# Cross attention with a recurrent layer behind it: score steps of a light kind, the second norm in the same iteration, the shift ahead of the spread on the queue

## The reference

```python
q, k, v = x @ Wq + bq, ctx @ Wk + bk, ctx @ Wv + bv       # heads of 8
attn = softmax(q k^T / sqrt(8) + mask)
x = norm(concat(attn v) @ Wo + bo + x) * gamma + beta
xa = ln1(x); sx = previous row of xa - xa
xxx = tanh((xa + sx * maa_x) @ maa_w1)                    # 5 x 32 wide
xk, xw, xv, xr, xg = xa + sx * (maa_stack + xxx @ maa_w2)
w = exp(-exp(time_decay + tanh(xw @ td_w1) @ td_w2))
r, k, v, g = xr @ Wr.T, xk @ Wk.T, xv @ Wv.T, silu(xg @ Wg.T)
def step(s, (r, k, v, w)):                                # over 256 tokens
    a = outer(k, v); return a + w * s, r @ (u * a + s)
x1 = x + (groupnorm(out) * gn_w + gn_b) * g @ Wo.T
xc = ln2(x1); sx2 = previous row of xc - xc               # the second norm
rr = sigmoid((xc + sx2 * ffn_maa_r) @ Wfr.T)
kk = relu((xc + sx2 * ffn_maa_k) @ Wfk.T) ** 2
return x1 + rr * (kk @ Wfv.T)
```

## Time and profile before

| what | value |
|---|---|
| three runs, median (lowest to highest) | 1322.82 us (1318.57 to 1328.49) |
| the profiled execution's own time | 1320.78 us |
| its span, first to last instruction | 1319.0 us |
| PE busy in the span | 1055.0 us (80%) |
| ACT busy | 867.8 us (66%) |
| DVE busy | 633.2 us (48%) |
| POOL busy | 295.0 us (22%) |
| granted clock of PE, mean | 0.919 |

### The profile page before, as it was taken

The page is one execution under the profiler, slowest core; times in us unless marked ns, Lnnn a source line. Parts: engine busy times, 40 slices in busy tenths (PEclk is TensorE's granted clock), DMA queues, the critical chain, the costliest instruction groups (busy, mean ns, idle before and its releaser), DMA issues.

```text
span 1319.0 us, 18192 instructions
## 1 busy us (share of the span) xinstructions
PE 1055.0 (80%) x7100; PEld 388.9 (29%) x7100; DVE 633.2 (48%) x1113; ACT 867.8 (66%) x953; POOL 295.0 (22%) x333
## 2 busy tenths in 40 slices
PE   3067788888898989989898989898988789876654
PEld 1022222332333323322333233332332234213412
DVE  5313122565454735384366536474547334734373
ACT  1047888767776788768776777678866888683001
POOL 6103104121221304130413032230413011301130
PEclk9579999989988999889999998899999999898766
DMA  6543213270326123341327131703241022200210
GB/s 188 127 130 101 62 52 78 44 134 11 85 66 132 25 75 85 50 105 52 72 53 139 41 60 61 143 15 87 72 69 30 2 40 39 44 1 0 42 31 10
DMA packets 65565, 87.47 MB, mean 66 GB/s; under 512 B 8208, under 2 KB 48192, under 8 KB 65472
## 3 DMA queue, kind: packets, MB, share of 16 engines
q1 hardware_dynamic: 63536, 82.91, 29.3%
q0 software_dynamic: 1936, 3.32, 0.9%
HBM read 50.74 MB, written 18.62 MB: 53 GB/s over the span
## 4 chain that ended last, share of the span: by engine, by line
PE 48%; ACT 16%; issue 15%; DVE 15%; POOL 3%; DMA 1%; SPq 1%; ACTq 0%; POOLq 0%; DVEq 0%
PE psum L708 47%; ACT probs L647 13%; DVE vs L1274 2%; DVE row_max L1161 2%; DVE vs L1281 2%; DVE mask_max L1156 1%; DVE k_stack L1491 1%; DVE tmp L1422 1%; ACT L647 1%; DMA vs<-v_c 1%; DVE xa L1248 1%; SPq L328 1%; DMA q_stack<-q_stacked 1%; POOL k_rest L500 0%; DVE sx L1253 0%
## 5 line engine op out<-in xcount | busy, mean ns | idle before, releaser
L647 ACT ACTIVATE probs<-psum 128x1024 f32<-128x1024 f32 (+1 forms) x832 | 797.3, 1024 | 314.7 <-PE psum L708 312.8
L708 PE MATMUL psum<-probs,v_aug 128*9 128x512 f32 (+1 forms) x3328 | 421.3, 618 | 1.1 <-ACT probs L647 0.9
L708 PE MATMUL psum<-q_stack,k_stack 64*128 64x512 bf16 (+1 forms) x1664 | 279.7, 393 | 135.1 <-ACT probs L647 95.6
L708 PEld LDWEIGHTS psum<-q_stack,k_stack 64*128 64x128 bf16 (+1 forms) x1664 | 65.4, 95 | 439.8 <-ACT probs L647 338.4
L708 PEld LDWEIGHTS psum<-probs,v_aug 128*9 128x9 f32 (+1 forms) x3328 | 71.6, 91 | 202.3 <-issue 177.0
L552 POOL TENSOR_TENSOR vs<-r_c,vs 128x512 f32<-128x512 f32 x64 | 84.0, 1318 | 151.6 <-DVE r_c L1418 78.4
L1161 DVE TENSOR_REDUCE row_max<-psum 128x8 f32<-128x1024 f32 x64 | 78.0, 1218 | 59.0 <-PE psum L708 57.7
L1281 DVE TENSOR_TENSOR_SCAN vs<-w_c,vs 128x514 f32<-128x514 f32 x64 | 100.3, 1567 | 12.0 <-POOL vs L543 10.1
L535 POOL TENSOR_TENSOR xm<-tmp,xa 128x512 f32<-128x512 f32 x40 | 46.0, 1166 | 247.9 <-DVE tmp L1268 247.9
L522 POOL TENSOR_TENSOR rstd<-moments,eps 128x2 f32<-128x2 f32 x24 | 4.9, 206 | 311.2 <-DVE moments L1234 311.1
L1208 DVE COPY o_raw<-psum 128x512 f32<-128x512 f32 x32 | 22.1, 689 | 102.8 <-PE psum L708 102.8
(11 more groups left out here) (175 smaller groups left out, 1089.1 us busy)
## 6 DMA issues: line engine op xcount, KB each, us to landing
vs<-v_c SPq DMA_DIRECT2D x64, 257.0 KB, 7.2
ctx_t<-in_mask SPq DMA_DIRECT2D x8, 1601.0 KB, 6.6
k_stacked<-k_parts SPq DMA_DIRECT2D x48, 200.1 KB
k_stack<-k_stacked SPq DMA_DIRECT2D x32, 300.2 KB, 6.6
ctx_t<-in_ctx_t SPq DMA_DIRECT2D x24, 400.0 KB, 5.2
q_stacked<-q_parts SPq DMA_DIRECT2D x96, 64.0 KB, 2.0
q_stack<-q_stacked SPq DMA_DIRECT2D x32, 192.0 KB, 7.3
ctx_t<-in_ctx_t SPq DMA_DIRECT2D x8, 401.0 KB, 3.6
```

Of the source, the lines that this page charges most:

```text
L647: nc.scalar.activation(probs[turn_step % NP][t][0:w, :, :], ps[t][0:w, :, :], ACT.Exp).then_inc(exped.sem, 1)
L708: return nc.tensor.matmul(dst, lhsT, rhs, start=start, stop=stop)
```

## The change

Four things are altered. (1) In the pairs that begin at a step of `LIGHT` (2, 8, 10, 18, 38, 42, 48), and in iteration 0 in all pairs but the first and those of `DIVIDED`, each weighing stands between the two score tiles of its step, where before both stood between the steps. (2) The second norm is done at the end of the iteration of `c`: PE turns `xn` at step 48 and multiplies by `Wfr` at step 50, POOL takes `root(c, 2)` last, DVE forms `xr2` and then `xk2`; `Wfk` follows at step 0 of the next iteration, relu and square on ACT at step 2, `Wfv` at step 6. What is left in `side` moves two steps ahead (four for `Wfv`), on ACT too: `h` from 14 to 12, `Wv` from 18 to 16, `Wr` from 26 to 24, `Wo` from 46 to 44, the queries from 48 to 46. The rounds of `b` move from steps 12 to 15 to 9 to 12, those of `a` by one. DVE's order follows. (3) On SP `shift_to_stack` of half 1 stands right behind `shift_to_dram`, ahead of `spread_v`. (4) `first_state` works on two states at a time, `read_out` waits for `rk`, and DVE makes state pass 3 before `r_c` and `rk`. The number of matmuls, exponentials and DMAs does not change. The core of the diff (the step numbers that only go down by two are left out):

```diff
 KV_SECOND = (5, 6, 5, 6)
...
-B_ROUNDS = [12, 13, 14, 15]
+KV_STEP = [30, 32, 40, 40]
+A_ROUNDS = [31, 32, 33, 34]
+B_ROUNDS = [9, 10, 11, 12]
 
 
...
-                        if step == 18 and b is not None:
+                        if step == 16 and b is not None:
                             shift_to_dram(b, 1)
-                        if step == 20 and c is not None:
+                            shift_to_stack(b, 1)
+                        if step == 18 and c is not None:
                             spread_v(c)
-                        if step == 20 and b is not None:
-                            shift_to_stack(b, 1)
...
-                j0, j1 = HD // 2 * part, HD // 2 * (part + 1)
+                j0, j1 = 2 * part, 2 * part + 2
...
+                pool.wait_ge(rk_ready.sem, rk_ready.at(c))
                 for j in range(HD):
-                    if j == 2:
-                        first_state(c, 1)
+                    if j in (2, 4):
+                        first_state(c, j // 2 + 1)
                     pool.wait_ge(s_ready.sem, s_ready.at(c, j + 1))
...
                     f, a, b, c, d = elements(it, lo)
-                    if d is not None:
...
                         first_state(c, 0)
+                        first_state(c, 1)
                         mixed(c, 4)
...
+                    if c is not None:
+                        root(c, 2)
...
-                    if step == 6:
+                    if step == 2:
                         act.wait_ge(kk_done.sem, kk_done.at(d))
-                        nc.scalar.activation(kk_relu[:, :, :], halves(6), ACT.Relu).then_inc(kk_relued.sem, 1)
+                        nc.scalar.activation(kk_relu[:, :, :], halves(7), ACT.Relu).then_inc(kk_relued.sem, 1)
...
-                    if step == 10:
+                    if step == 0:
                         act.wait_ge(rr_done.sem, rr_done.at(d))
-                        nc.scalar.activation(rr_tanh, halves(7), ACT.Tanh, scale=0.5).then_inc(rr_ready.sem, 1)
+                        nc.scalar.activation(rr_tanh, halves(6), ACT.Tanh, scale=0.5).then_inc(rr_ready.sem, 1)
...
-                if d is not None and step == 0:
-                    pe.wait_ge(xn2_ready.sem, xn2_ready.at(d))
-                    if a is not None:
-                        pe.wait_ge(q_scaled.sem, q_scaled.at(a))
-                    turn_rows(xn, 7, xt2_turned)
                 if c is not None:
-                    if step == 2:
-                        if d is not None:
-                            pe.wait_ge(std_ready.sem, std_ready.at(d))
+                    if step == 0:
+                        pe.wait_ge(o_normed.sem, o_normed.at(c, 3))
                         turn_output(c, 3, 5)
...
-                    elif step == 6:
+                    elif step == 4:
                         pe.wait_ge(attn_kept.sem, attn_kept.at(c))
                         product_rows(attn_t, w_o, 5, wo_done)
-                    elif step == 14:
+                    elif step == 10:
+                        pe.wait_ge(xn_ready.sem, xn_ready.at(c))
+                        turn_rows(xn, 5, xt_turned)
...
+                    elif step == 48:
+                        pe.wait_ge(xn2_ready.sem, xn2_ready.at(c))
+                        if f is not None:
+                            pe.wait_ge(q_scaled.sem, q_scaled.at(f))
+                        turn_rows(xn, 7, xt2_turned)
+                    elif step == 50:
+                        pe.wait_ge(xr2_ready.sem, xr2_ready.at(c))
+                        pe.wait_ge(x1_ready.sem, x1_ready.at(c))
+                        product_rows(xr2, wsq["Wfr"], 6, rr_done)
                 if d is not None:
-                    if step == 4:
+                    if step == 0:
                         pe.wait_ge(xk2_ready.sem, xk2_ready.at(d))
-                        pe.wait_ge(x1_ready.sem, x1_ready.at(d))
-                        product(wsq["Wfk"], xk2, 6, kk_done)
-                    elif step == 8:
-                        pe.wait_ge(xr2_ready.sem, xr2_ready.at(d))
+                        product(wsq["Wfk"], xk2, 7, kk_done)
...
+                        pe.wait_ge(kk_ready.sem, kk_ready.at(d))
+                        pe.wait_ge(rr_ready.sem, rr_ready.at(d))
                         if a is not None:
                             pe.wait_ge(v_kept.sem, v_kept.at(a, 1))
...
-                        product_rows(xr2, wsq["Wfr"], 7, rr_done)
-                    elif step == 10:
-                        pe.wait_ge(kk_ready.sem, kk_ready.at(d))
-                        if a is not None:
-                            pe.wait_ge(v_kept.sem, v_kept.at(a))
                         product_rows(kk_c, wsq["Wfv"], 6, ff_done)
-                if c is not None and step == 10:
-                    pe.wait_ge(xn_ready.sem, xn_ready.at(c))
-                    turn_rows(xn, 5, xt_turned)
...
+                        light = step in LIGHT or (c is None and step > 0 and step not in DIVIDED)
                         if b is not None:
                             score_tile(b, step, 0, general)
+                            if light:
+                                weigh(b, step - 2)
                             score_tile(b, step, 1, general)
                         score_rows(step - 1, it, lo, general)
                         if step == 0:
                             if c is not None:
                                 weigh(c, STEPS - 2)
                                 weigh(c, STEPS - 1)
-                        elif b is not None:
+                        elif b is not None and not light:
                             weigh(b, step - 2)
                             if step not in DIVIDED:
                                 weigh(b, step - 1)
                         if b is not None:
                             score_tile(b, step + 1, 0, general)
+                            if light:
+                                weigh(b, step - 1)
                             score_tile(b, step + 1, 1, general)
                         score_rows(step, it, lo, general)
...
-                dve.wait_ge(s_begun.sem, s_begun.at(c, 2 * j // HD + 1))
+                dve.wait_ge(s_begun.sem, s_begun.at(c, j // 2 + 1))
...
-                    if d is not None:
-                        scaled_rows(xn, x1, d, 2).then_inc(xn2_ready.sem, 1)
...
@@ -1345,53 +1344,50 @@
                             see_mask(a, 1)
                     if c is not None:
                         keep_output(c, 3)
-                    if d is not None:
-                        dve.wait_ge(xt2_turned.sem, xt2_turned.at(d))
-                        token_differences(d, 0, 7, "ln2_w", "ln2_b")
-                        shift_mix(xk2, "ffn_maa_k", xk2_ready)
-                        shift_mix(xr2, "ffn_maa_r", xr2_ready)
-                    if c is not None:
                         norm_output(c, 3, 5)
-                    if it > lo and a is not None:
-                        keep_v(a, 0, 7)
-                    if c is not None:
                         dve.wait_ge(attn_turned.sem, attn_turned.at(c))
                         nc.vector.tensor_copy(attn_t[:, :, :], halves(5)).then_inc(attn_kept.sem, 1)
+                    if it > lo and a is not None:
+                        keep_v(a, 0, 6)
+                        if not general:
+                            see_mask(a, 0)
+                    if c is not None:
                         dve.wait_ge(xb_ready.sem, xb_ready.at(c))
                         dve.wait_ge(wo_done.sem, wo_done.at(c))
                         nc.vector.tensor_tensor(x0[:, :, :], halves(5), x_rows[:, :, :], ALU.add).then_inc(x0_ready.sem, 1)
                         dve.wait_ge(x0_ready.sem, x0_ready.at(c))
                         row_moments(x0, c, 0)
-                    if it > lo and a is not None:
-                        keep_v(a, 1, 6)
-                    if c is not None:
                         link(scaled_rows(x0, x0, c, 0))
...
+                    if it > lo and a is not None:
+                        keep_v(a, 1, 7)
+                    if c is not None:
                         row_moments(x0, c, 1)
+                    if d is not None:
+                        write_out(d)
                     if it == B and not general:
                         count_over()
                         raise_flag()
...
-                    if it > lo and a is not None and not general:
-                        see_mask(a, 0)
-                    if d is not None:
-                        write_out(d)
+                    if b is not None:
+                        reduce_step(b, 1, 0, general)
+                        reduce_step(b, 1, 1, general)
                     if c is not None:
                         dve.wait_ge(xt_turned.sem, xt_turned.at(c))
                         token_differences(c, 1, 5, "ln1_w", "ln1_b")
+                    if b is not None:
+                        reduce_step(b, 1, 2, general)
+                    if c is not None:
```

(17 more changed lines are left out.)

136 lines of the change are left out of this document (64 added, 72 removed).

## The result

The changed kernel takes 1244.23 us (median of four runs, 1242.85 to 1248.33), the kernel before in the same session 1324.08 (1318.57 to 1328.49): a ratio of 0.940, 95% interval 0.936 to 0.945. The forecast was 1245.

A forecast was written before the change was run, and what follows sets the result against it. PE was taken to set the pace, busy 127.8 of 143.1 us; terms sum to -7.75 us per full iteration and 78 us overall, giving 1245 us. The forecast's own range was 1228 to 1262, the wider one 1212 to 1284.

The forecast's parts named there:

- queue wait: PE's wait at the first score tile of step 26, for a small transfer queued behind the spread, goes: -4.55 us.
- clock: Slow matmuls behind PE's gaps cost 3.2 us an iteration; half of one 1.6 us stretch stays: -2.4 us.
- exponentials and split tiles: In light pairs PE's waits for exponentials fall from 8.8 to 5.1 us (-3.7); fewer split tile pairs and gaps give -1.0.
- DVE and POOL: New PE waits for norms, rounds of b, h and mixes make 6.2 us against 1.1 + 1.1 + 0.1 before: +3.9.
- The rule on initiating a DMA: On SP's queue, initiation is usually small relative to the DMA, so queue place would be worth nothing; 14.92 us speaks against it.
- (a): DVE from k_c's copy to the second output norm: waits 0.8 and 1.2 us; rk's 1.96 gain and scan 4's 1.4 to 2 loss count zero.
- (c): Second norm at the iteration's end, Wo to r_c, against PE's 11.9 us before Wfr: 0 counted, 2.8 us upper end.
- the slower rival: PE meets Wfr at step 50 with the 16.6 us chain bare seven times: a loss of 38, 1360 us; chance 0.04.
- Iterations: Gains by iteration: 0, 10 us; 1, 9.5; 2 to 5, 31; 6, 9; 7, 12; the end 6.5.
- Rival 1: DVE's idle time covers the new waits, costing 2 rather than 6.2 us in six iterations: 1220 us; chance 0.2.
- rival 2: DVE and POOL become the bound between steps 9 and 14 and 24 and 30: +28, 1273 us; chance 0.17.
- Rival 3: The step 26 wait was not the queue's place, or another load takes its turn: 43 back, 1288 us; chance 0.06.

The follow-up runs named there:

- the queue alone: The kernel before with only the shift's transfer to the stack rows issued right behind its way to DRAM, ahead of the eight spread DMAs: 1281.98 us, 0.969.
- relu behind step 4: The changed kernel with ACT's relu and square of the second half behind the tiles of step 4 instead of light pair 2: 1243.95 us, 0.939.
- the root ahead of the keys: The changed kernel with POOL's two roots for c put ahead of the key split: 1261.75 us, 0.953.

## Why the prediction held, step by step

The number was right within a microsecond, and that is partly luck: of its terms, several were off and cancelled. The range and the chain of causes held; the closeness says little. For a full period (third one, in us):

| term | forecast | measured | from |
|---|---|---|---|
| queue wait | -4.55 | -4.2 to -4.4 | "issue" 5.5 to 5.7 before, 1.3 with the queue alone |
| clock | -2.4 | about -4.6; mean of iterations 1 to 7: -2.3 | PE busy 127.8 to 123.25, queue alone |
| exponentials and split tiles | -4.7 | -2.8 | 136.60 without light pairs, 133.80 with |
| DVE and POOL | +3.9 | +2.3 | 1.1 of new waits with the queue alone; 1.2 from all else of the change, 136.60 less 135.36 |
| sum | -7.75 | -9.3 | 143.1 to 133.8 |

- **The queue.** The mechanism was right: the transfer stood behind the spread, and in the kernel before its place alone is worth 42 us, against 43 by the forecast's terms. The step that failed is "the spread itself is not delayed ... that distance does not change". The distance that mattered was from the spread to step 26, and in the changed kernel, where `Wv` comes two steps earlier, it is 5.7 us longer. I credited the whole wait to the queue's order, and in the changed kernel that order is worth nothing (1243.37 with it undone). The total came out right because the wait can be removed only once.
- **The rule on initiating a DMA.** The queue's place alone took 42 us off the kernel before, and nothing off the changed one. The Trainium skill, "DMA: Bandwidth & Descriptors", section "Issuing engines are not separate DMA queues", calls the time to initiate a DMA usually small relative to the DMA itself. Read as the prediction read it, both would be nothing; the 42 us do not agree with that, since eight issues in a row add up to 14.9 us.
- **The clock.** Mis-sized for this period: I kept half of one slow stretch for the new small gaps, and there was none. The granted clock was 1.00, with waits of 0.57 to 1.20 still in it. But the same small waits can have a slow stretch behind them. Behind the waits of 1.03 and 0.52 in the second period, and of 1.03 and 0.53 in the third, stand these weighings:

```profile
341.91 2.96 PE L710 MATMUL psum<-probs,v_aug 128*9 128x512 f32 x16
...
475.25 1.91 PE L710 MATMUL psum<-probs,v_aug 128*9 128x512 f32 x16
```

  Over iterations 1 to 7 the queue's edit alone took 16.3 us off PE's busy time, 2.3 each, so on the mean the term was right. The term for split tiles (-1.0) does not show: in a period without a slow weighing or `mix`, PE is busy for 123.25 us with the queue alone and for 125.18 in the changed kernel, presumably because light pairs split rows too.
- **Exponentials.** The waits themselves were forecast at 5.1 and are 3.6 in eight (8.8 before). The two largest, 1.03 and 0.53 behind pair 2, stand where the prediction put 1.75. The period gained less than the waits fell: without light pairs the exponentials' waits are 7.5, and of the 3.9 less, 1.1 came back as waits for row maxima.
- **DVE and POOL.** `Wr` 0.8 and the projection 1.2 were forecast; 0.76 and 1.20 came, which agrees with the count of DVE's work in a row. The rounds of `b`, `h` and the mixes were put at 3.7 and sum to 2.5 (0.57, 0.68, 0.27, 0.19, 0.29, and 0.52 for ACT). The root began right behind the key split, as forecast (484.80), and DVE waited 4.39 for it, where the forecast had it 3.2 late (its own figures, 23.5 less 20, give 3.5). What I left out is why the key split is late: POOL idles 4.23 us for the rows of `x` in front of it, and 4.16 in the kernel before, where it could have been read.
- **(a) `rk` and scan 4.** Counted as zero. `rk` takes 0.87 instead of 2.84, as read; scan 4 waits 2.42 for POOL's first state, more than the 1.4 to 2 counted.
- **(c) `Wfr`.** No wait in the full periods, so the slower rival had no ground. Only the last one, in the end, waits 2.81 for its input.
- **Iterations.** Iteration 0 was forecast at -10 and gave -9.5 (light pairs are all of it: 202.71 without them). Iterations 1 to 7 gave 58.5 for 61.5, with the four full ones better (34.1 for 31) and iterations 6 and 7 worse (6.5 for 9, 8.4 for 12; the changed kernel has slow weighings of 3.16 to 3.53 in them). The end gave 8.7 for 6.5; the first scan's wait fell from 4.98 to 0.18, while scan 4 there waits 2.40:

```profile
1175.58 1.23 DVE L1282 TENSOR_TENSOR_SCAN vs<-w_c,vs 128x514 f32<-128x514 f32 x1 [0.18 <-POOL vs L544]
...
1188.78 2.12 DVE L1282 TENSOR_TENSOR_SCAN vs<-w_c,vs 128x514 f32<-128x514 f32 x1 [2.40 <-POOL vs L544]
```

- **The rivals.** Rival 1 (waits covered, 1220) and rival 2 (DVE and POOL the bound, 1273) were both about the size of one term. That term came out at +2.3 for a forecast of +3.9, so a part of rival 1 is true, and it is hidden in the total by iterations 6 and 7. Rival 3 is refuted for the kernel before by the queue alone, and true of the changed one in the sense above.

What stays open: how much of the queue's 42 us belongs to the two earlier steps if they stood alone in the kernel before. That was not tried; that they suffice together with the rest of the change follows from the changed kernel with the queue's order undone.

## What to carry to other kernels

When a change holds two edits that could each remove the same wait, forecast the wait once and measure both single edits; undoing one in the final version can cost nothing and still leave it the right edit elsewhere. Follow a late instruction back past the busy engine in front of it to the first idle time of its chain: here a root behind a split of 9.5 us was late by a DMA that stood behind four others, and the fix was to move one line of a queue. An edit that removes a wait ahead of a fixed chain shows nothing until the chain is moved too (relu behind step 4: nothing alone, and by difference some 7 of 30.7 us together), so a null result for one edit is not yet a verdict on it.

## What the runs showed of the hardware

- Behind the issue of four context loads (1.6 MB) and one of 256 KB, the tile that needs two transfers of 12 KB started 4.2 to 5.7 us after the end of their issue; behind the eight spreads, 1.7 to 1.9.
- Two row operations of DVE with a tile in SBUF took 4.90 us beside POOL's conversion and subtraction of 64 x 1601, instead of 0.73.
- Behind the gap at step 26 (4.3 to 4.9 us) the next weighing took 2.86 to 3.60 us for 1.90 in all seven iterations of the kernel before. The granted clock of such a period was 0.95, 0.96 and once 0.99.
- Slow rows also stand behind small waits, and not every time: 2.96 for 1.90 behind waits of 1.03 and 0.52 in the second period of the changed kernel, none behind 1.03 and 0.53 in the third. In the kernel with the root ahead of the keys (3.88 us gap, granted clock 0.96) one of two slow weighings, 3.23 at 476.62, stands ahead of that gap. So the longest gap of a period does not fix its clock, and what does stays open.
